# First attention of a four-block fp32 kernel: its heads taken four at a time instead of two, with the product with V split in three

## Chip, core and metric

The kernel runs on one core of a Trainium2 chip. The metric is the device time in microseconds (us), and smaller is better. Every time here is from runs of the kernel, or from one profiled execution of it.

## What is computed

The input x is four sequences of 512 tokens by 512 channels, all fp32. Four residual blocks follow one another: causal attention with 16 heads of 32 channels, a feed-forward with ternary weights, a selective scan, and a last block with a second attention and a mixture of experts. The change is in the first attention:

```python
qkv = jnp.einsum('btc,oc->bto', x, W_qkv).reshape(B, T, 3, H, D)
...
q = _rms_norm(q * cos + _rotate_half(q) * sin)
k = _rms_norm(k * cos + _rotate_half(k) * sin)
scores = jnp.einsum('bhqd,bhkd->bhqk', q, k) * scale
scores = jnp.where(causal[None, None], scores, jnp.float32(-1000000000.0))
attn = jax.nn.softmax(scores, axis=-1)
out = jnp.einsum('bhqk,bhkd->bqhd', attn, v)
out = jnp.transpose(out, (0, 2, 1, 3)).reshape(B, T, C)
return jnp.einsum('btc,oc->bto', out, W_o)
```

## The kernel before, in words

One sequence goes through all layers in a pass of `step`, and there are four passes. Pass 0 has no routed experts to work on; in its place DVE, POOL and the DMA queue turn the feed-forward's weights into ternary ones, from thresholds that need sums over all of those weights. Passes 1 to 3 are one body in a hardware loop; in them the experts of the sequence before run beside the layers of this one. Every engine has its own written-out order of work, and semaphores tie them together. The weights of the q, k and v projection (`wqkv`, 24 KB in each partition) lie in slots 0 and 1 of `ring`; slot 2 holds the shared expert. Once v is there (`v_done`), SP loads the first two routed experts over slots 0 and 1.

The first attention works on pairs of heads, eight pairs (`p`). The heads of a pair lie in two of the four groups of 32 partitions of QT and KT. The scores are transposed (keys in the partitions) and causal: key tile 0 has 512 query columns, tiles 1 to 3 have 384, 256 and 128. They lie in three units: tile 0; tiles 1 and 3; tile 2.

- PE, `pe_A_scores` (L601): for each unit, the matmuls of both heads, each into its own PSUM bank, six banks in all. A unit waits for the exp of the same unit of the pair before.
- ACT (L1620): exp of each unit of two banks into PT, which has room for two pairs.
- POOL, `p_A_select` (L1880): after the third exp it zeroes what lies above the diagonal, in two instructions.
- PE, `pe_A_pv` (L618): the product with V, and with ones for the denominators, of both heads in two column groups, once the select is done. PE does scores of pair p, then the product of pair p-1.
- DVE, `v_A_pair` (L1102 to L1113): transposes the sums, takes reciprocals, and writes two heads to AOT. In pass 0 DVE also has a sum of absolute values of one weight chunk (L1188) after each of the first seven turns.

After the last product PE has, in passes 1 to 3, a part of the shared expert (`pe_E_part`, L910) and then the output projection (`pe_project_A`, L528), which waits for all eight pairs of DVE. In pass 0 the total of the sums (L1158, then the matmul L570 into bank 7) comes before the last product, because the thresholds wait for it; POOL and DVE quantise after it (L1214, L1225).

An fp32 matmul is two instructions on PE here, each with its own weight load (PEld).

```python
for p in range(NP):
    pe_A_scores(pe, p)
    if p:
        pe_A_pv(pe, p - 1)
...
square = PT[:, n % 2].rearrange("p x (k q) -> p (x k) q", q=P)
for blocks in (square[:, 7::12], square[:, 0:21:4]):
```

Of the kernel before, what the change touches and what calls it, by code (L numbers as in the profile page):

```python
# [20 lines left out]
F32 = mybir.dt.float32  # L21
# [8 lines left out]
P = 128  # L30
B, T, C = 4, 512, 512
NT = T // P
# [95 lines left out]
def build(nc, x_in, pack_in, packb_in, wqkv_in, tern_in, exp_in, tern_q, xg, yg, out):  # L128
# [9 lines left out]
    def at(name, shape, dtype, reg, off=0):  # L138
        return nc.alloc_sbuf_tensor_at(name, shape, dtype, offset=offs[reg] + off)
# [77 lines left out]
    STK = at("STK", [P, 4, 2 * GH, 4, HD], F32R, "arena", 40 * KB)  # L217
    QT = at("QT", [P, NK, T], F32, "arena", 24 * KB)
    KT = at("KT", [P, NK, T], F32, "arena", 32 * KB)
    PT = at("PT", [P, 2, 2, 3 * T], F32, "arena", 40 * KB)  # L220
    RA = at("RA", [P, T], F32, "arena", 8 * KB)
    TD = at("TD", [P, T], F32, "arena", 0)
    RDEN = at("RDEN", [P, 16], F32, "arena", 2 * KB)
# [86 lines left out]
    with ExitStack() as ctx:  # L310
# [159 lines left out]
        def tile(i):  # L470
            return slice(i * P, (i + 1) * P)
# [66 lines left out]
        def pe_A(pe, experts):  # L538
            for i in range(NT):
                if i == 1 and experts:  # L540
                    pe_logits(pe)
                if i == 2 and experts:
                    pe_counts(pe)
                if i >= 2:
                    pe.wait_ge(rope_parts, 3 * (i - 1))
                    pe.wait_ge(qk_squared, i - 1)
                pe_A_qkv(pe, i, 0)
                pe_A_qkv(pe, i, 1).then_inc(qk_done, 1)

            for i in range(NT):  # L550
                if i == 1 and experts:
                    pe.wait_ge(r_idx, 1)
                if i >= 2:
                    pe.wait_ge(v_copied, i - 1)
                pe_A_qkv(pe, i, 2).then_inc(v_done, 1)
                if i == 2:
                    for j in range(NT - 1):
                        pe_A_qk(pe, j)
            pe_A_qk(pe, NT - 1)
            for z in range(2):  # L560
                t_emptied(pe, ("qk", NT - 1, z))
            pe.wait_ge(v_copied, NT)
            for p in range(NP):
                pe_A_scores(pe, p)
                if p:
                    pe_A_pv(pe, p - 1)
            if not experts:
                pe.wait_ge(abs_sums, 1)
                pe.wait_ge(a_exp, 3 * NP)
                pe.matmul(ps[:, 7, 0:3], ONES[:], SABS[:], start=True, stop=True).then_inc(thr_sum, 1)  # L570
            pe_A_pv(pe, NP - 1)
            if experts:
                pe.wait_ge(a_exp, 3 * NP)
                pe_E_part(pe, 0, 0, 0, NK)
            else:
                pe.wait_ge(late_loaded, 16)
            pe_project_A(pe)
# [11 lines left out]
        def heads_of(p):  # L589

            g, o = divmod(p, 2)
            return [(4 * g + r, slice(32 * r, 32 * r + 32)) for r in (o, o + 2)]

        def pe_A_scores(pe, p):
            for unit, (_, col, width) in enumerate(A_UNIT):
                if p:
                    pe.wait_ge(a_exp, 3 * (p - 1) + unit + 1)
                for kt in (k for k in range(NT) if A_PLACE[k][0] == unit):
                    off = A_PLACE[kt][1] - col
                    for x, (h, rows) in enumerate(heads_of(p)):  # L600
                        last = pe.matmul(ps[:, 2 + 2 * unit + x, off:off + T - kt * P], KT[rows, h // 4, tile(kt)],  # L601
                                         QT[rows, h // 4, kt * P:T], start=True, stop=True)
                last.then_inc(a_scores, 1)

        def v_ones(h, kt):

            return VA[:, kt, h // 2, h % 2:h % 2 + 2].rearrange("p a d -> p (a d)")

        def pe_A_pv(pe, p):
            if p == 0:  # L610
                pe.wait_ge(ones_a, 1)
            pe.wait_ge(a_sel, p + 1)
            if p >= 2:
                pe.wait_ge(a_head, p - 1)
            for kt in range(NT):
                for x, (h, _) in enumerate(heads_of(p)):
                    col = A_PLACE[kt][1]
                    last = pe.matmul(ps[64 * x:64 * x + 64, p % 2, kt * P:T], v_ones(h, kt),  # L618
                                     PT[:, p % 2, x, col:col + T - kt * P], start=(kt == 0), stop=(kt == NT - 1),
                                     skip_group_check=True)  # L620
            last.then_inc(a_pv, 1)

        def h_bank(m):
            return 2 * (1 - m % 2)
# [472 lines left out]

        def v_A_pair(v, p):

            v.wait_ge(a_pv, p + 1)  # L1100
            odd = p % 2
            v.transpose(TD[:], ps[:, odd]).then_inc(a_recip, 1)  # L1102
            v.wait_ge(a_recip, 3 * p + 1)
            v.reciprocal(RDEN[:], TD[:].rearrange("p (k r) -> p k r", r=32)[:, :, 0]).then_inc(a_recip, 1)
            v.wait_ge(a_recip, 3 * p + 2)
            if p:
                v.wait_ge(a_head, p)
            v.transpose(RA[:].rearrange("p (k r) -> p k r", r=32),
                        RDEN[:].rearrange("p (k o) -> p k o", o=1).to_broadcast([P, 16, 32])).then_inc(a_recip, 1)
            v.wait_ge(a_recip, 3 * p + 3)  # L1110
            for h, rows in heads_of(p):
                den = slice(rows.start + 32 - 64 * odd, rows.stop + 32 - 64 * odd)
                ins = v.tensor_tensor(AOT[rows, h // 4], ps[rows, odd], RA[den], ALU.mult)  # L1113
            ins.then_inc(a_head, 1)

        def v_A(v, experts):
# [481 lines left out]
        def s_A(s, experts):  # L1598
            for i in range(NT):
                b0 = 2 + 3 * (i % 2)  # L1600
                s.wait_ge(qk_done, i + 1)
                if i:
                    s_rms(s, i - 1)
                s.activation(SQ[:], ps[:, b0:b0 + 2, :].rearrange("p b (h d) -> p (b h) d", d=HD),
                             ACT.Square).then_inc(qk_squared, 1)
                if i == 0 and experts:
                    s_route(s)
            s_rms(s, NT - 1)
            for i in range(NT):
                s_v(s, 0, i)  # L1610
                if i == 2:
                    for j in range(NT - 1):
                        s_copy_bank(s, ("qk", j, 0), QT[:, :, tile(j)])
            s_copy_bank(s, ("qk", NT - 1, 0), QT[:, :, tile(NT - 1)])
            for p in range(NP):
                for unit, (_, col, width) in enumerate(A_UNIT):
                    s.wait_ge(a_scores, 3 * p + unit + 1)
                    if p >= 2:
                        s.wait_ge(a_pv, p - 1)
                    s.activation(PT[:, p % 2, :, col:col + width], ps[:, 2 + 2 * unit:4 + 2 * unit, 0:width], ACT.Exp,  # L1620
                                 scale=SCALE).then_inc(a_exp, 1)
            if experts:
                s_tanh(s, 0)
# [251 lines left out]
        def p_A_select(p, n):  # L1875

            p.wait_ge(a_exp, 3 * (n + 1))
            square = PT[:, n % 2].rearrange("p x (k q) -> p (x k) q", q=P)
            for blocks in (square[:, 7::12], square[:, 0:21:4]):
                ins = p.affine_select(blocks, blocks, [[0, blocks.shape[1]], [1, P]], ALU.is_ge, 0.0, base=0, channel_multiplier=-1)  # L1880
            ins.then_inc(a_sel, 1)

# [25 lines left out]
        def p_A(p, link, experts):  # L1908
            p.memset(VA[:, :, :, 1], 1.0).then_inc(ones_a, 1)
            if experts:  # L1910
                p_scatter(p)
            for n in range(NP):
                p_A_select(p, n)
            if not experts:
                for m in range(2):
                    p_below(p, m)
            for i in range(NT):
                p_rstd(p, link, 1, i)
            if not experts:
                for m in range(2, NM):  # L1920
                    p_below(p, m)
# [161 lines left out]
        def step(x_next, out_batch, experts):  # L2083
# [10 lines left out]
            with nc.Block() as block:  # L2094
                @block.sync
                def _(sp):
# [5 lines left out]
                            n = min(NT, NB - b)  # L2102
                            sp.dma_start(rows[:, b:b + n], XS[:, 0:n]).then_inc(zeros_sent, 16)
                    if experts:
                        sp.wait_ge(v_done, NT)
                        for b in range(2):
                            load_gate_up(sp, b, exp_in[b + 1])
                            load_down(sp, b, exp_in[b + 1])
                        sp.wait_ge(a_pv, NP)
                        for m in range(NM):  # L2110
                            load_tern(sp, m)
                        xs_all_sent(sp)
                        sp.wait_ge(e_up, 2)
# [20 lines left out]
                    else:  # L2134
                        sp.dma_start(ring[:, 2], exp_in[0]).then_inc(next_loaded, 16)
                        load_next(sp)
                        sp.wait_ge(next_loaded, 16)
                    if experts:
                        sp.wait_ge(stored, 16)
                        sp.wait_ge(wqkv_loaded, 16)  # L2140
                    sp.wait_ge(x_loaded, 16 * NT)

                @block.tensor
# [189 lines left out]
```

## Time and profile before

| what | us |
| --- | --- |
| median of 3 runs (2122.47 to 2124.69) | 2123.91 |
| the profiled execution, its own time | 2125.45 |
| span of its instructions | 2123.7 |
| PE busy | 1885.2 (89%) |
| DVE busy | 1377.2 (65%) |
| ACT busy | 994.7 (47%) |
| POOL busy | 786.7 (37%) |
| mean granted TensorE clock | 0.928 |

Times in the trace count from the start of the span. PE is TensorE's matmuls, PEld its weight loads, DVE VectorE, ACT ScalarE, POOL GpSimd, SP the engine that issues DMAs. What stands in brackets behind a row is the idle time of its engine before it, and who ended it. A granted clock of 1.0 is 2.4 GHz, and 0.5 is 1.2 GHz. The first attention's scores begin at 67.5 us in pass 0 and at 568.7 us in pass 1.

### The profile page before, as it was taken

The numbers are of one execution on the slowest core, as the hardware profiler recorded it, in microseconds if no ns is written. First come the engines' busy times: TensorE is split into PE (matmuls) and PEld (weight loads), VectorE is DVE, ScalarE is ACT, GpSimd is POOL, SyncE is SP. The second block draws the span as 40 slices with busy tenths as digits, with TensorE's granted clock in tenths as the row PEclk, the third lists the DMA queues.
The fourth block names the chain that finished last, engine by engine and source line by source line (L and its number), as shares of the span: only waits on it lengthen the run. The fifth ranks groups of instructions, "written<-read, shape, count | busy, mean of one in ns | idle before, by whom it ended". The sixth has DMA issues, their size and how long they took to land. (4 is left out here: it accounts for less than half of the span.)

```text
span 2123.7 us, 27520 instructions
## 1 busy us (share of the span) xinstructions
PE 1885.2 (89%) x9226; PEld 1238.9 (58%) x9226; DVE 1377.2 (65%) x2196; ACT 994.7 (47%) x1736; POOL 786.7 (37%) x1057
## 2 busy tenths in 40 slices
PE   7878665998999899997999899898899999899895
PEld 3446443695458565695447555496446666588442
DVE  5766698574563799574664699577554499667411
ACT  1412774462322786363232698264142399355021
POOL 1146377441210276561120177372020157472201
PEclk9989755998999999998999999999899999899898
DMA  6337100000213185200213176210022257310683
GB/s 259 109 115 245 52 0 20 1 2 1 99 45 119 57 266 173 96 25 22 79 51 119 35 244 227 84 41 21 17 97 93 69 175 263 127 41 21 237 311 104
DMA packets 55072, 221.09 MB, mean 104 GB/s; under 512 B 6288, under 2 KB 6288, under 8 KB 46992
## 3 DMA queue, kind: packets, MB, share of 16 engines
q1 hardware_dynamic: 45776, 195.14, 26.5%
q0 software_dynamic: 5120, 16.78, 2.4%
q10 hardware_dynamic: 4032, 7.34, 0.9%
q8 instruction: 80, 1.31, 0.3%
q14 instruction: 64, 0.52, 0.1%
HBM read 179.65 MB, written 39.58 MB: 103 GB/s over the span
## 5 line engine op out<-in xcount | busy, mean ns | idle before, releaser
L1933 POOL TENSOR_TENSOR Y<-Y,HC 128x1024 f32<-128x1024 f32 x116 | 273.9, 2362 | 174.0 <-DVE HC L1336 173.4
L1325 DVE TENSOR_TENSOR_SCAN HS<-DA,ps 128x1024 f32<-128x1024 f32 x128 | 292.3, 2284 | 23.5 <-PE ps L742 13.0
L534 PE MATMUL ps<-ring,XNT 128*128 128x512 f32 x384 | 182.4, 633 | 21.0 <-issue 12.2
L1688 ACT ACTIVATE DA<-DL,AB,AN 128x511 f32<-128x511 f32 x256 | 193.8, 806 | 14.8 <-DVE HS L1325 13.5
L954 PE MATMUL ps<-ring,XBT 128*128 128x512 f32 x384 | 188.5, 597 | 0.0
L1801 ACT ACTIVATE PD<-ps,NMX 128x128 f32<-128x128 f32 (+3 forms) x256 | 135.1, 530 | 101.2 <-DVE NMX L1470 99.2
L1470 DVE TENSOR_REDUCE NMX<-ps 128x1 f32<-128x128 f32 (+3 forms) x256 | 124.3, 487 | 65.4 <-PE ps L805 65.1
L823 PE MATMUL ps<-V,PTD 128*128 128x33 f32 x1280 | 164.2, 262 | 0.0
L823 PEld LDWEIGHTS ps<-V,PTD 128*128 128x128 f32 x1280 | 162.6, 192 | 0.5 <-ACT PTD L839 0.5
L650 PE MATMUL ps<-XNH,tern 128*128 128x512 f32 x352 | 139.2, 396 | 9.8 <-DVE tern L1225 5.4
L534 PEld LDWEIGHTS ps<-ring,XNT 128*128 128x128 f32 x384 | 76.6, 204 | 117.4 <-issue 108.1
L1336 DVE TENSOR_TENSOR HC<-HS,ps 128x1024 f32<-128x1024 f32 x120 | 143.2, 1196 | 0.0
L650 PE MATMUL ps<-XNL,tern 128*128 128x512 f32 x352 | 137.9, 392 | 0.0
L1847 POOL TENSOR_SCALAR RS<-MV 128x1 f32<-128x1 f32 x32 | 12.8, 399 | 291.7 <-DVE MV L1039 291.7
L1872 POOL TENSOR_TENSOR STK<-QN,STK 128x128 fp32r<-128x128 f32 x256 | 116.4, 476 | 10.3
L1868 POOL CAST STK<-QN 128x128 fp32r<-128x128 f32 x256 | 67.9, 295 | 139.4 <-DVE QN L1460 90.5
L814 PE MATMUL ps<-pack,PD 128*128 128x128 f32 x640 | 113.4, 275 | 4.3 <-ACT XNT L1082 4.3
L742 PE MATMUL ps<-pack,UBE 128*128 128x128 f32 x512 | 84.5, 320 | 26.1 <-DVE HS L1325 22.8
L1620 ACT ACTIVATE PT<-ps 128x1024 f32<-128x1024 f32 (+1 forms) x96 | 77.3, 886 | 57.0 <-PE ps L601 57.0
L803 PE MATMUL ps<-QKS 128*128 128x128 f32 (+3 forms) x256 | 99.8, 392 | 3.1 <-ACT QKS L1076 3.1
L1880 POOL TENSOR_SCALAR_AFFINE_SELECT PT<-PT 128x256 f32<-128x256 f32 x64 | 39.3, 638 | 169.8 <-ACT PT L1620 169.8
L742 PE MATMUL ps<-pack,UBO 128*128 128x128 f32 x512 | 81.4, 313 | 21.6 <-DVE HS L1325 20.5
(248 smaller groups left out, 4026.0 us busy)
## 6 DMA issues: line engine op xcount, KB each, us to landing
ring<-experts_dram SPq DMA_DIRECT2D x48, 1024.0 KB, 5.1
tern<-tern_q SPq DMA_DIRECT2D x33, 768.0 KB, 4.2
ring<-experts_dram SPq DMA_DIRECT2D x48, 512.0 KB, 5.4
RAW<-tern_dram SPq DMA_DIRECT2D x22, 768.0 KB, 4.8
ring<-wqkv_dram SPq DMA_DIRECT2D x4, 3072.0 KB, 11.9
XB<-xg SPq DMA_DIRECT2D x42, 256.0 KB, 3.6
yg<-YB SPq DMA_DIRECT2D x42, 256.0 KB, 4.9
tern_q<-tern SPq DMA_DIRECT2D x11, 768.0 KB, 7.0
```

The lines of the kernel that those rows point to most:

```text
L534: last = pe.matmul(ps[:, 2 + 3 * (i % 2) + part], XNT[:, k, tile(i)], wqkv[:, k, part * C:(part + 1) * C], start=(k == 0), stop=(k == NK - 1))
L650: last = pe.matmul(ps[:, h_bank(m) + n], tern[:, m % 3, w:w + P], parts[a][:, k], start=(k + a == 0), stop=(k == NK - 1 and a == 1))
L742: last = pe.transpose(ps[:, 2 * q + jj, tile(i)], ub(n, i)[:, tile(2 * q + jj)], ident)
L823: last = pe.matmul(ps[:, 6 + h % 2, 33 * i:33 * i + 33], PTD[:, v % 3, tile(kt)], V1[:, kt, h], start=(kt == 0), stop=(kt == i))
L954: last = pe.matmul(ps[:, g_bank(b)], XBT[:, b % 2, k], weights(b)[:, k * C:(k + 1) * C], start=(k == 0), stop=(k == NK - 1), skip_group_ch ...
L1325: v.tensor_tensor_scan(HS[:, q].rearrange("p j t -> p (j t)"), DA[:, q].rearrange("p j t -> p (j t)"), ps[:, 2 * q:2 * q + 2].rearrange("p ...
L1336: v.tensor_tensor(dst, HS[:, q], ps[:, 4:5, :].to_broadcast([P, 2, T]), ALU.mult).then_inc(c_hc, 1)
L1470: v.tensor_reduce(NMX[:, u % 4:u % 4 + 1], ps[:, 2 + u % 3, 0:(i + 1) * P], AX.X, ALU.max, negate=True).then_inc(d_max, 1)
L1688: s.activation(DA[:, u % 2, jj, 1:T], DL[:, j, 1:T], ACT.Exp, scale=AN[:, j * NS + n:j * NS + n + 1], bias=AB[:, j * NS + n:j * NS + n + 1 ...
L1801: s.activation(PD[:, u % 3, 0:(i + 1) * P], ps[:, 2 + u % 3, 0:(i + 1) * P], ACT.Exp, bias=NMX[:, u % 4:u % 4 + 1]).then_inc(d_exp, 1)
L1872: p.tensor_tensor(st[:, :, LOW[z]], qn, st[:, :, HIGH[z]].bitcast(F32), ALU.subtract).then_inc(stack_ready, 1)
L1933: p.tensor_tensor(y, y, HC[:, q], ALU.add).then_inc(c_y, 1)
```

## The change

The unit of work becomes a quad of four heads (`g`, four quads), in all four groups of partitions. The scores of one unit go to the four banks 2 to 5, and all three units share these banks, so each unit waits for the exp of the unit before it. The exps work on four banks at a time. The product with V of quad g-1 is cut by unit and set between the score units of quad g; it goes to banks 6 and 7 or 0 and 1 in turn. The select of a quad is four instructions, after its third exp. DVE still works by pairs, but gets two pairs at once. PT becomes two buffers of 24 KB; the second lies in slots 0 and 1 of `ring`. So the first two experts are loaded later (behind the third chunk of ternary weights), and pass 0 loads `wqkv` again at its end. The total of the absolute sums in pass 0 comes after the last product.

```diff
-    PT = at("PT", [P, 2, 2, 3 * T], F32, "arena", 40 * KB)
+    PT = (at("PT0", [P, 4, 3 * T], F32, "arena", 40 * KB), at("PT1", [P, 4, 3 * T], F32, "ring"))
...
-            for p in range(NP):
-                pe_A_scores(pe, p)
-                if p:
-                    pe_A_pv(pe, p - 1)
+            for g in range(NK + 1):
+                for unit in range(len(A_UNIT)):
+                    if g < NK:
+                        pe_A_scores(pe, g, unit)
+                    if g:
+                        pe_A_pv(pe, g - 1, unit)
             if not experts:
                 pe.wait_ge(abs_sums, 1)
-                pe.wait_ge(a_exp, 3 * NP)
+                pe.wait_ge(a_head, NP - 2)
                 pe.matmul(ps[:, 7, 0:3], ONES[:], SABS[:], start=True, stop=True).then_inc(thr_sum, 1)
-            pe_A_pv(pe, NP - 1)
             if experts:
-                pe.wait_ge(a_exp, 3 * NP)
+                pe.wait_ge(a_head, NP - 2)
                 pe_E_part(pe, 0, 0, 0, NK)
...
+        def a_bank(g):
+            return 6 * (1 - g % 2)
+
+        def pe_A_scores(pe, g, unit):
+
+            if g or unit:
+                pe.wait_ge(a_exp, 3 * g + unit)
+            _, col, width = A_UNIT[unit]
+            for kt in (k for k in range(NT) if A_PLACE[k][0] == unit):
+                off = A_PLACE[kt][1] - col
+                for r in range(4):
+                    rows = slice(32 * r, 32 * r + 32)
+                    last = pe.matmul(ps[:, 2 + r, off:off + T - kt * P], KT[rows, g, tile(kt)],
+                                     QT[rows, g, kt * P:T], start=True, stop=True)
+            last.then_inc(a_scores, 1)
...
+        def pe_A_pv(pe, g, unit):
+            if unit == 0:
+                if g == 0:
+                    pe.wait_ge(ones_a, 1)
+                pe.wait_ge(a_sel, g + 1)
+                if g >= 2:
+                    pe.wait_ge(a_head, 2 * (g - 1))
+            for kt in (k for k in range(NT) if A_PLACE[k][0] == unit):
+                for o in range(2):
+                    for x in range(2):
+                        col = A_PLACE[kt][1]
+                        last = pe.matmul(ps[64 * x:64 * x + 64, a_bank(g) + o, kt * P:T], v_ones(4 * g + o + 2 * x, kt),
+                                         PT[g % 2][:, o + 2 * x, col:col + T - kt * P], start=(kt == 0), stop=(kt == 2),
+                                         skip_group_check=True)
+            if unit == len(A_UNIT) - 1:
+                last.then_inc(a_pv, 1)
...
-            v.wait_ge(a_pv, p + 1)
+            v.wait_ge(a_pv, p // 2 + 1)
...
-                    s.activation(PT[:, p % 2, :, col:col + width], ps[:, 2 + 2 * unit:4 + 2 * unit, 0:width], ACT.Exp,
+                    s.activation(PT[g % 2][:, :, col:col + width], ps[:, 2:6, 0:width], ACT.Exp,
...
-            for blocks in (square[:, 7::12], square[:, 0:21:4]):
+            for blocks in (square[:, 7::12], square[:, 0::12], square[:, 4::12], square[:, 8::12]):
...
                     if experts:
-                        sp.wait_ge(v_done, NT)
-                        for b in range(2):
-                            load_gate_up(sp, b, exp_in[b + 1])
-                            load_down(sp, b, exp_in[b + 1])
-                        sp.wait_ge(a_pv, NP)
+                        sp.wait_ge(a_pv, NK)
                         for m in range(NM):
+                            if m == 3:
+                                for b in range(2):
+                                    load_gate_up(sp, b, exp_in[b + 1])
+                                    load_down(sp, b, exp_in[b + 1])
                             load_tern(sp, m)
...
                         load_next(sp)
+                        sp.dma_start(wqkv[:], wqkv_in.rearrange("p (k n) -> p k n", k=NK)).then_inc(wqkv_loaded, 16)
```

## Rows read from the trace of the kernel before

**Rows 1.** The page's busy times: engine, us, share of the span, instructions.

```profile
PE 1885.2 (89%) x9226; PEld 1238.9 (58%) x9226; DVE 1377.2 (65%) x2196; ACT 994.7 (47%) x1736; POOL 786.7 (37%) x1057
```

**Rows 2.** Timeline, pass 1, one pair: start, us, engine, line, operation [idle before].

```profile
585.35 2.43 PE L601 MATMUL ps<-QT,KT 32*128 32x512 f32 x16
...
586.53 2.43 ACT L1620 ACTIVATE PT<-ps 128x1024 f32<-128x1024 f32 x3 [2.23 <-PE ps L601]
...
587.71 2.37 PE L618 MATMUL ps<-PT,VA 128*64 128x512 f32 x16
...
589.02 1.23 POOL L1880 TENSOR_SCALAR_AFFINE_SELECT PT<-PT 128x256 f32<-128x256 f32 x2 [3.44 <-ACT PT L1620]
...
590.02 2.43 PE L601 MATMUL ps<-QT,KT 32*128 32x512 f32 x16
```

**Rows 3.** Groups by form, pass 1, 568 to 611 us: busy us, mean ns | idle before.

```profile
L1620 ACT ACTIVATE PT<-ps 128x1024 f32<-128x1024 f32 x16 | 15.5, 1025 | 14.2 <-PE ps L601 14.2
...
L1880 POOL TENSOR_SCALAR_AFFINE_SELECT PT<-PT 128x768 f32<-128x768 f32 x8 | 6.9, 866 | 0.0
...
L1620 ACT ACTIVATE PT<-ps 128x512 f32<-128x512 f32 x8 | 4.9, 608 | 0.0
...
L601 PE MATMUL ps<-QT,KT 32*128 32x256 f32 x32 | 4.8, 376 | 0.0
...
L1880 POOL TENSOR_SCALAR_AFFINE_SELECT PT<-PT 128x256 f32<-128x256 f32 x8 | 3.3, 410 | 31.7 <-ACT PT L1620 31.7
...
L601 PE MATMUL ps<-QT,KT 32*128 32x128 f32 x32 | 3.1, 269 | 0.0
```

**Rows 4.** Timeline, pass 1, the first two pairs' scores.

```profile
568.68 4.72 PE L601 MATMUL ps<-QT,KT 32*128 32x512 f32 x32 [0.83 <-DVE KT L1082]
```

**Rows 5.** Timeline, pass 1, the end of the first attention.

```profile
604.12 0.72 DVE L1102 STREAM_TRANSPOSE TD<-ps 128x512 f32<-128x512 f32 x1 [1.48 <-PE ps L618]
...
606.59 3.70 PE L910 MATMUL ps<-XET,ring 128*128 128x512 f32 x8
...
607.32 0.72 DVE L1102 STREAM_TRANSPOSE TD<-ps 128x512 f32<-128x512 f32 x1
...
610.55 10.57 PE L528 MATMUL ps<-pack,AOT 128*128 128x512 f32 x24 [0.26 <-DVE AOT L1113]
```

**Rows 6.** Timeline, pass 0, DVE and PE.

```profile
74.96 0.72 DVE L1102 STREAM_TRANSPOSE TD<-ps 128x512 f32<-128x512 f32 x1 [5.79 <-PE ps L618]
...
105.60 0.72 DVE L1102 STREAM_TRANSPOSE TD<-ps 128x512 f32<-128x512 f32 x1
...
108.80 0.19 DVE L1158 TENSOR_REDUCE SABS<-SPART 128x3 f32<-128x33 f32 x1
...
113.60 0.72 DVE L1102 STREAM_TRANSPOSE TD<-ps 128x512 f32<-128x512 f32 x1 [3.25 <-PE ps L618]
...
116.92 13.53 PE L528 MATMUL ps<-pack,AOT 128*128 128x512 f32 x24 [3.45 <-DVE AOT L1113]
```

**Rows 7.** Timeline of PE: three places where it had been idle.

```profile
716.01 0.66 PE L712 MATMUL ps<-pack,U 128*128 128x128 f32 x4 [2.66 <-DVE U L1285]
...
883.26 1.50 PE L495 MATMUL ps<-pack,STK 128*128 128x128 f32 x12 [1.62 <-DVE M L1455]
...
1484.05 0.66 PE L488 MATMUL ps<-pack,XS 128*128 128x128 f32 x4 [2.21 <-DVE XS L1046]
```

**Rows 8.** Stretches: us, busy times (instructions) by engine, granted clock, DMA share, GB/s.

```profile
716.90:727.10 10.20, 8.03 (x36) 7.41 (x37) 6.83 (x4) 10.17 (x19) 1.71 (x2) 0.50 0.09 23
...
1485.00:1498.00 13.00, 5.65 (x10) 2.65 (x11) 1.44 (x2) 2.20 (x3) 1.10 (x2) 0.50 0.02 6
...
883.00:897.00 14.00, 11.05 (x92) 9.71 (x92) 8.80 (x20) 7.40 (x15) 12.11 (x31) 1.00 0.14 40
256.00:370.00 114.00, 65.58 (x255) 48.99 (x256) 106.34 (x75) 73.58 (x112) 84.49 (x51) 0.50 0.03 10
```

**Rows 9.** Stretch in which the first two experts are loaded, pass 1; columns as above.

```profile
572.00:575.00 3.00, 2.68 (x22) 1.38 (x22) 0.00 (x0) 2.60 (x4) 1.57 (x3) 1.00 1.03 425
```

More of the change, by code:

```diff
@@ L592, in heads_of @@
             return [(4 * g + r, slice(32 * r, 32 * r + 32)) for r in (o, o + 2)]
[L594 to L603, printed above, removed]
+        def a_bank(g):
+            return 6 * (1 - g % 2)
@@ L605, in v_ones @@
         def v_ones(h, kt):
             return VA[:, kt, h // 2, h % 2:h % 2 + 2].rearrange("p a d -> p (a d)")
[L609 to L621, printed above, removed]
+        def pe_A_pv(pe, g, unit):
[14 more added lines that the diff above has]
+                last.then_inc(a_pv, 1)
@@ L1098, in v_A_pair @@
         def v_A_pair(v, p):
-            v.wait_ge(a_pv, p + 1)
+            v.wait_ge(a_pv, p // 2 + 1)
             odd = p % 2
-            v.transpose(TD[:], ps[:, odd]).then_inc(a_recip, 1)
+            bank = a_bank(p // 2) + odd
+            v.transpose(TD[:], ps[:, bank]).then_inc(a_recip, 1)
             v.wait_ge(a_recip, 3 * p + 1)
@@ L1112, in v_A_pair @@
                 den = slice(rows.start + 32 - 64 * odd, rows.stop + 32 - 64 * odd)
-                ins = v.tensor_tensor(AOT[rows, h // 4], ps[rows, odd], RA[den], ALU.mult)
+                ins = v.tensor_tensor(AOT[rows, h // 4], ps[rows, bank], RA[den], ALU.mult)
             ins.then_inc(a_head, 1)
@@ L1614, in s_A @@
             s_copy_bank(s, ("qk", NT - 1, 0), QT[:, :, tile(NT - 1)])
-            for p in range(NP):
+            for g in range(NK):
                 for unit, (_, col, width) in enumerate(A_UNIT):
-                    s.wait_ge(a_scores, 3 * p + unit + 1)
-                    if p >= 2:
-                        s.wait_ge(a_pv, p - 1)
-                    s.activation(PT[:, p % 2, :, col:col + width], ps[:, 2 + 2 * unit:4 + 2 * unit, 0:width], ACT.Exp,
+                    s.wait_ge(a_scores, 3 * g + unit + 1)
+                    if g >= 2:
+                        s.wait_ge(a_pv, g - 1)
+                    s.activation(PT[g % 2][:, :, col:col + width], ps[:, 2:6, 0:width], ACT.Exp,
                                  scale=SCALE).then_inc(a_exp, 1)
@@ L1877, in p_A_select @@
             p.wait_ge(a_exp, 3 * (n + 1))
-            square = PT[:, n % 2].rearrange("p x (k q) -> p (x k) q", q=P)
-            for blocks in (square[:, 7::12], square[:, 0:21:4]):
+            square = PT[n % 2][:].rearrange("p x (k q) -> p (x k) q", q=P)
+            for blocks in (square[:, 7::12], square[:, 0::12], square[:, 4::12], square[:, 8::12]):
                 ins = p.affine_select(blocks, blocks, [[0, blocks.shape[1]], [1, P]], ALU.is_ge, 0.0, base=0, channel_multiplier=-1)
@@ L1911, in p_A @@
                 p_scatter(p)
-            for n in range(NP):
+            for n in range(NK):
                 p_A_select(p, n)
@@ L2139, in _ @@
                         sp.wait_ge(stored, 16)
-                        sp.wait_ge(wqkv_loaded, 16)
+                    sp.wait_ge(wqkv_loaded, 16)
                     sp.wait_ge(x_loaded, 16 * NT)
```

## The prediction

> **What bounds the kernel now.** I read the page's busy times first: PE is busy for 89% of the span, so it is the engine to watch [rows 1]. Then I read the timeline of one pair in pass 1, where the reader is to see a closed loop on PE: scores begin at 585.35, the product with V at 587.71, the next scores at 590.02, with no idle time [rows 2]. A pair takes 4.67 us, four heads take 9.33, and ACT waits 2.23 us in each pair for PE. The exps (2.43 us) and the select (1.23 us) run under PE's work. So cheaper scores can pay only if what hides behind them stays hidden. The groups by form give the prices [rows 3], the rows at the stage's two ends show what PE waits for after it [rows 4, 5], and pass 0 is a case of its own: from 74.96 to 105.60 DVE works through six turns of 5.11 us without waiting, so there DVE is the bound, and the thresholds and the last pair follow it [rows 6].
>
> **Prices.** 128 more columns cost an fp32 scores matmul 376 - 269 = 107 ns, for each of its two instructions [rows 3]. A head has 1280 columns, so two heads side by side need 10 x 2 x 0.107 = 2.14 us. Scores took 2.36 and the product 2.31 [rows 2], so each change between the two array shapes costs about 0.2. ACT sees a 512-column unit 1.18 us after its first matmul [rows 2], and a 256-column one after some 0.75 (0.1 shape, 0.21 first instruction, 0.38 the last one's own time, 0.05 signal). Exp costs 608 ns for 512 elements and 1025 for 1024 [rows 3]: 0.81 per 1000 and 0.19 fixed, so 1.86 for four banks of 512 (a quad's first two units) and 1.02 for the third. Select costs 410 ns for 256 elements and 866 for 768 [rows 3], so 0.64 for 512; four of them, overlapping as now, take 2.45.
>
> **Scores in four row groups.** The trace shows two groups side by side and not four. Bounds: four cost what two cost (2.14 a quad instead of 4.28), or they run as two and two (4.28). I take the first, since the second head now adds nothing that shows. On this the Trainium skill speaks against the full gain: "TensorE: Matmul & The Clock Gate", section "Measured speedup vs the span model", gives 3.07 times for four row tiles of K=32, N=512. An estimate from that page's figure is scores 1.30 times as long, 0.7 us a quad, 11 us over the kernel; no row here shows it, and the sum leaves it out.
>
> **The new cycle.** The three score units share four banks, so exp and scores alternate. Let an exp chain of a quad end at 0. At 0.05 the next quad's first scores start, and their exp starts at 1.23 and ends at 3.09. The select of the old quad runs from 0.06 to 2.51. PE has its scores done at 1.0 and then stands before the product until 2.55, because that waits for the whole select, which nothing covers now. The product's first part ends at 4.3 (two banks x 2 x 0.43, and 0.05). Scores of unit 1 are queued behind it: 4.4, exp from 5.58 to 7.44. Product part 2 lies beside that exp (5.4 to 7.2). Scores of unit 2 start at 7.5, exp 8.25 to 9.27. The cycle is 9.3 us against 9.33 before: **the 2.14 us that scores save are given back** to the select (1.5), the exp waits (0.3) and two more shape changes (0.4).
>
> **The ends of the stage.** Quad 0 has no product beside it: 3.04, 3.09 and 1.8 us for its three units, 7.95 in all. Three cycles follow, to 35.8. Then the last select, bare, to 38.3. Then a whole quad's product, 4.28 + 0.1: 42.7. DVE gets pairs 6 and 7 together; a pair takes 607.32 - 604.12 = 3.20 [rows 5], so the last head is there at 42.7 + 0.2 + 6.4 = 49.3. Before, the projection began 610.55 - 568.68 = 41.9 after the first scores [rows 4, 5]. **The stage ends 7.4 us later**, in passes 1 to 3. The shared expert's part (3.7 us, rows 5 show it beside the last pair) fills less of the wait. I take 7.3, as ideal joins may lose or save 0.1.
>
> **Clock.** What PE did before its clock fell: after idle times of 2.66 and 2.21 us it stood at 0.50 (1.2 GHz) for the next 10.2 and 13 us; after one of 1.62 between dense work it stayed at 1.00 (2.4 GHz) [rows 7, 8]. The new stage has such idle times at three places that had none. (a) Quad 0: 2 us, 2 us and 1 us with about 1 us of work between. Price: nothing, up to 5 (10.2 us at half); PE's waits absorb part, and I take 1.4. (b) Before the last product: PE's work ended at 35.6, so 2.7 us idle, as the row that fell: the product's 4.4 us become 8.6, +4.2 (bounds 0 and 5.1). (c) Before the projection: PE is through with the expert's part at about 51.6, DVE at 53.5; 1.9 us lie between the row that fell and the one that did not, so I take half of 5.1, 2.5.
> Passes 1 to 3: 7.3 + 1.4 + 4.2 + 2.5 = 15.4 each, 46.2.
>
> **Pass 0.** DVE has nothing to do until the first quad's product is done, at 17.0 + 0.2 + 1.4 (a): 67.5 + 18.6 = 86.1 in place of 74.96, and its queue is in order, so the sums of later chunks wait too. Six turns of 5.11 end at 116.8, pair 6 at 120.0; sum, its matmul and thresholds 1.5 (the same work as before, now with pair 7 behind it), pair 7: 124.7. Before, pair 7 started at 113.60 and ended at 116.8. +7.9. The projection is slow there already (24 matmuls in 13.53 us against 10.57 [rows 5, 6]), so its clock adds nothing. The quantising waits for thresholds that come 11 us later, but its second chunk ends by 132, as the first residual add would start: hidden, up to 1.
>
> **DMA and the rest.** The first two experts, 3 MB, now follow the third ternary chunk; they moved at 425 GB/s [rows 9], so 8 us. The fourth chunk, queued behind them on SP, is asked for only after the first down product; in the code two norms, two up products and that one lie between, longer than the 8 us. Cost 0, and if that cover went, up to 3 a pass. The experts themselves are needed only in the scan. The second load of wqkv has the last attention of pass 0 over it: 0. Addresses and banks: 0.
>
> **Sum.** 46.2 + 7.9 = 54.1. The profiled execution took 2125.45, so it would be 2179.6; it stands 1.5 above the median of 2123.91, and against that I say **2178**.
>
> **Rivals.**
> - *Schedule only, no fall of the clock.* 3 x 7.3 + 6.5 = 28.4: 2152. For it: score bursts in quad 0 may count as work. Against: idle times over 2.2 us were followed by 0.50 in both rows.
> - *Four groups run as two and two.* The change would not do what it says. Every 512-column unit is 0.43 later; by the same steps the stage is 6 longer (3.4 in pass 0, where only the first two quads count): +21, 2199.
> - *The clock stays low through the stage,* as in pass 0's scan, at 0.50 for 114 us with PE busy 58% [rows 8]. Product and scores at half, 14.5 a quad: about 20 more a pass: 2240. Against: at half speed PE has hardly a gap left, and there it recovers.
> - *Faster.* One mechanism: the shift in time takes away low-clock stretches elsewhere, such as those after 716 and 1484 us [rows 8], each worth 5.1 to 6.5. The stage alone loses 28 even without new falls (a cycle below 6.9 us would be needed to break even, and PE's own work is 7.6), so it takes six stretches gone and none new: about 2117 with seven. I know of no reason why.
> - *Select much cheaper and no fall:* with 1.2 us in place of 2.45 the cycle is 8.1 and the end 1.2 earlier: 4.8 less a pass, 2135. Even that is slower.
>
> **How the numbers follow.** Forecast 0.55 (its own range 2160 to 2196), schedule only 0.2, two and two 0.1, low throughout 0.05, cheap select 0.03, faster 0.05, no change 0.02. The range goes from 2143, below schedule only, to 2205, above two and two. A difference under 0.2% (4 us) can't be told from none here. Faster 0.05, same 0.02, slower 0.93.
>
> **What would show it.** Right: PE rows of a quad 9.3 us apart; idle of 1.5 us before the first product part, ended by POOL; 2.7 us before the last; scores of a quad begun within 30 ns in four groups; exps of 1.86; DVE pairs 6 and 7 back to back and the projection 49 us or more after the first scores; granted clock 0.50 over the last product. In pass 0, thresholds some 11 us later. Wrong: a cycle under 8.5, a select under 1.5 in all, or the clock at 1.00 through the stage's end (then 2152).

## The result, and the profile after

The changed kernel is slower: median 2164.77 us of four runs (2162.29 to 2170.81) against 2123.19 of the kernel before, ratio 1.0205 with a 95% interval of 1.0177 to 1.0233 (the two medians alone give 1.0196). So that it is slower is clear, and whether by more than 2% is not. The profiled execution has a span of 2169.0 us against 2123.7, so 45.3 more.

| first scores to start of projection, us | before | after | forecast |
| --- | --- | --- | --- |
| pass 0 | 49.4 | 57.2 | +7.9 |
| pass 1 | 41.9 | 52.2 | +15.4 less 2.5 (c, in the projection) |
| pass 2 | 41.9 | 53.8 | the same |
| pass 3 | 41.8 | 53.8 | the same |

These four lines hold 42.0 of the 45.3: 7.8 + 10.3 + 11.9 + 12.0. The rest lies outside (the first scores 1.3 later in pass 0; from each projection to the next pass's scores +3.3, +3.4 and -4.8; the end +0.1). The -4.8 says little of the change: the kernel before itself took 446.4 us there in pass 1 and 452.8 in pass 2, and its low-clock stretches lie differently in the two.

The page's busy times answer to [rows 1]. PE is busy for 9 us less, yet the span is 45 longer.

```profile
PE 1876.5 (87%) x9226; PEld 1222.6 (56%) x9226; DVE 1378.0 (64%) x2196; ACT 993.9 (46%) x1688; POOL 783.6 (36%) x1057
```

One cycle of a quad, in the timeline of pass 2 after the change; it answers to [rows 2].

```profile
1103.06 1.14 PE L607 MATMUL ps<-QT,KT 32*128 32x512 f32 x8
1103.07 2.40 POOL L1890 TENSOR_SCALAR_AFFINE_SELECT PT<-PT 128x512 f32<-128x512 f32 x4 [8.87 <-ACT PT L1630]
...
1104.27 1.88 ACT L1630 ACTIVATE PT<-ps 128x2048 f32<-128x2048 f32 x1 [1.26 <-PE ps L607]
...
1105.53 1.94 PE L626 MATMUL ps<-PT,VA 128*64 128x512 f32 x8 [1.33 <-POOL PT L1890]
...
1107.39 1.15 PE L607 MATMUL ps<-QT,KT 32*128 32x384 f32 x16
...
1108.47 1.95 PE L626 MATMUL ps<-PT,VA 128*64 128x384 f32 x16
1108.61 1.88 ACT L1630 ACTIVATE PT<-ps 128x2048 f32<-128x2048 f32 x1 [2.47 <-PE ps L607]
...
1110.54 0.71 PE L607 MATMUL ps<-QT,KT 32*128 32x256 f32 x8
1111.18 1.08 PE L626 MATMUL ps<-PT,VA 128*64 128x256 f32 x8
...
1112.40 1.14 PE L607 MATMUL ps<-QT,KT 32*128 32x512 f32 x8
```

Read it from the first line: eight matmul instructions, four heads, are done in 1.14 us, and their exp starts 1.21 us after the first of them has begun, where with two heads it was 1.18 [rows 2]. The first four matmul instructions, one of each head, begin within 20 ns (1103.059 to 1103.079). So all four row groups ran side by side. Then look at the bracket before the first product: PE stood 1.33 us for POOL's select, which takes 2.40. The next quad starts 9.34 us after this one; two pairs took 9.33. The gain on scores is gone within the cycle.

The end of the stage in the same pass; it answers to [rows 5].

```profile
1121.65 0.72 DVE L1112 STREAM_TRANSPOSE TD<-ps 128x512 f32<-128x512 f32 x1 [2.96 <-PE ps L626]
1121.75 2.40 POOL L1890 TENSOR_SCALAR_AFFINE_SELECT PT<-PT 128x512 f32<-128x512 f32 x4 [6.94 <-ACT PT L1630]
...
1124.20 6.22 PE L626 MATMUL ps<-PT,VA 128*64 128x512 f32 x32 [2.60 <-POOL PT L1890]
...
1130.35 3.70 PE L919 MATMUL ps<-XET,ring 128*128 128x512 f32 x8
1130.47 0.72 DVE L1112 STREAM_TRANSPOSE TD<-ps 128x512 f32<-128x512 f32 x1 [2.44 <-PE ps L626]
...
1133.67 0.72 DVE L1112 STREAM_TRANSPOSE TD<-ps 128x512 f32<-128x512 f32 x1
...
1136.90 3.27 PE L528 MATMUL ps<-pack,AOT 128*128 128x512 f32 x7 [2.85 <-DVE AOT L1123]
```

The last select is bare (2.60 idle), the last product takes 6.22 us, then DVE's pairs 6 and 7 follow one another, and PE waits 2.85 for them. What PE waited for in the whole run (waiting line, releaser: us, times, longest):

```profile
PE ps L626 <- POOL PT L1890: 23.0, 16, 2.6
PE ps L607 <- ACT PT L1630: 20.5, 12, 2.0
```

The product waited for the select 16 times, once a quad. Before, both of its engines together (PE and its weight loads) had waited 3.3 us for it, in ten places.

The granted clock of four stretches of pass 2 (columns as in [rows 8]): quad 0; the three cycles; the last product; the projection.

```profile
1083.00:1092.00 9.00, 3.76 (x36) 1.81 (x40) 0.01 (x1) 5.60 (x4) 0.21 (x1) 0.77 0.01 2
1098.00:1123.00 25.00, 20.32 (x177) 9.15 (x176) 13.50 (x23) 12.46 (x8) 6.05 (x11) 1.00 0.00 1
1123.00:1131.00 8.00, 6.80 (x34) 2.98 (x35) 5.37 (x9) 0.00 (x0) 1.15 (x2) 0.79 0.01 2
1136.90:1147.00 10.10, 10.10 (x24) 4.60 (x25) 4.25 (x8) 0.00 (x0) 1.80 (x4) 1.00 0.00 0
```

The clock fell in quad 0 and in the last product, and not in the projection, though PE had been idle 2.85 us ahead of it. In pass 1 it was the other way: the last product took 4.53 us, and the projection's three tiles 12.26 in place of 10.57 [rows 5].

### The profile page after: what moved, and what is told of

Read it like the earlier page. It is cut to its first block and busy times, and to the rows that moved or that the text cites. A ratio compares the mean times of both kernels' runs of the same rounds, so it can differ in the third digit from the quotient of the medians.

```text
span 2169.0 us, 27409 instructions
## 1 busy us (share of the span) xinstructions
PE 1876.5 (87%) x9226; PEld 1222.6 (56%) x9226; DVE 1378.0 (64%) x2196; ACT 993.9 (46%) x1688; POOL 783.6 (36%) x1057
## 5 line engine op out<-in xcount | busy, mean ns | idle before, releaser
L1882 POOL TENSOR_TENSOR STK<-QN,STK 128x128 fp32r<-128x128 f32 x256 | 116.3, 476 | 10.3
L1630 ACT ACTIVATE PT<-ps 128x2048 f32<-128x2048 f32 (+1 forms) x48 | 76.5, 1593 | 73.7 <-PE ps L607 73.7
L626 PE MATMUL ps<-PT,VA 128*64 128x256 f32 (+3 forms) x512 | 88.4, 486 | 23.0 <-POOL PT L1890 23.0
L1890 POOL TENSOR_SCALAR_AFFINE_SELECT PT<-PT 128x512 f32<-128x512 f32 x64 | 38.4, 638 | 192.4 <-ACT PT L1630 192.4
```

What stands on the lines that cost most here:

```text
L1882: p.tensor_tensor(st[:, :, LOW[z]], qn, st[:, :, HIGH[z]].bitcast(F32), ALU.subtract).then_inc(stack_ready, 1)
```

## The experiments

### The select, by unit

```diff
-            p.wait_ge(a_exp, 3 * (n + 1))
             square = PT[n % 2][:].rearrange("p x (k q) -> p (x k) q", q=P)
-            for blocks in (square[:, 7::12], square[:, 0::12], square[:, 4::12], square[:, 8::12]):
-                ins = p.affine_select(...)
-            ins.then_inc(a_sel, 1)
+            for unit, offs_ in enumerate(((0,), (4, 7), (8,))):
+                p.wait_ge(a_exp, 3 * n + unit + 1)
+                for off in offs_:
+                    blocks = square[:, off::12]
+                    ins = p.affine_select(...)
+                ins.then_inc(a_sel, 1)
...
-                pe.wait_ge(a_sel, g + 1)
+            pe.wait_ge(a_sel, 3 * g + unit + 1)
```

> The changed kernel with its select cut by score unit: POOL masks unit 0 right after the first exp, the others after theirs, and each third of the product waits for its own select. Theory (the bare select of 2.4 us holds PE before the first third of the product, and the exp chain is the next limit): the cycle of a quad falls from 9.34 us to 8.0, the idle before the first third (1.33) goes, the idle of 2.6 before the last product falls to 0.7 or less; then DVE is late next, with pairs 4 to 7 back to back after the third quad's product, so the projection comes 4.5 to 6 us earlier in passes 1 to 3, and 1.3 in pass 0: some 18 us less than the change, ratio to the kernel before 1.012. Rival (the exp chain and the shape changes alone set 9.3): the cycle stays above 9, and less than 4 us are gained.

Measured: 2149.84 us, ratio 1.0122 (1.0100 to 1.0144). In passes 1 to 3 the projection starts 48.6 us after the first scores, 3.6 to 5.2 less than in the changed kernel. The timeline of pass 2:

```profile
1089.17 1.14 PE L607 MATMUL ps<-QT,KT 32*128 32x512 f32 x8
1090.24 1.94 PE L626 MATMUL ps<-PT,VA 128*64 128x512 f32 x8
...
1097.31 1.14 PE L607 MATMUL ps<-QT,KT 32*128 32x512 f32 x8
...
1105.37 0.72 DVE L1112 STREAM_TRANSPOSE TD<-ps 128x512 f32<-128x512 f32 x1 [1.76 <-PE ps L626]
...
1108.57 0.72 DVE L1112 STREAM_TRANSPOSE TD<-ps 128x512 f32<-128x512 f32 x1
...
1111.77 0.72 DVE L1112 STREAM_TRANSPOSE TD<-ps 128x512 f32<-128x512 f32 x1
1111.80 5.37 PE L919 MATMUL ps<-XET,ring 128*128 128x512 f32 x8 [2.17 <-DVE AOT L1123]
...
1114.97 0.72 DVE L1112 STREAM_TRANSPOSE TD<-ps 128x512 f32<-128x512 f32 x1
```

The product follows its scores with no idle time, the cycle is 8.14 us, and DVE now works through four pairs without a pause. The theory holds, its ratio of 1.012 too, and the rival falls: the bare select is 1.2 us of each cycle and more at the end. What is late next is DVE. The falls of the clock are still there (13.7 us at 0.50 in each of these stages); one makes the shared expert's part take 5.37 us in place of 3.70.

### Idle time filled with unread matmuls

```diff
+        def pe_fill(pe, n, bank):
+            for _ in range(n):
+                pe.matmul(ps[:, bank], KT[:, 0, tile(0)], QT[:, 0], start=True, stop=True)
...
+                    if g == 0:
+                        pe_fill(pe, (2, 2, 1)[unit], 7)
+                    if g == NK and unit == 0:
+                        pe.wait_ge(a_exp, 3 * NK)
+                        pe_fill(pe, 2, 2)
```

> The changed kernel with matmuls that nobody reads in PE's idle time: two after each of the first two score units of quad 0, one after the third, and two before the last product. They fit in the idle times (0.86 us each in 2.0, 2.0, 1.1 and 2.6 us), so the order and every wait stay. Theory (the idle times let the clock fall, and that costs 3 us in quad 0 and up to 1.7 before the last product, a pass): granted clock 1.00 over the whole stage, the projection 49.3 us after the first scores in place of 52.2 and 53.8, 3 to 4.6 us a pass and about 1 to 3 in pass 0, together 12 to 16 us less than the change: ratio 1.014. Rival (the clock falls in spite of them, or they push the chain): no gain, or 1 to 2 us more a pass.

Measured: 2162.73 us, ratio 1.0177 (1.0148 to 1.0207). Of the 12 to 16 us expected, 2 came by the medians and some 6 by the ratios, so the forecast of 1.014 missed. The stage did nearly what was forecast, 49.7 us in passes 1 to 3 in place of 52.2 and 53.8, with the clock at 1.00 in quad 0 and full speed in the last product; pass 0 gave 1.0. But the clock now fell over the projection in each of passes 1 to 3. Stretches of pass 2, quad 0 and projection, and the rows of the end:

```profile
1078.70:1088.00 9.30, 9.02 (x50) 3.30 (x50) 0.00 (x0) 5.48 (x4) 1.16 (x2) 1.00 0.01 2
1128.40:1138.00 9.60, 9.60 (x19) 4.37 (x20) 3.14 (x6) 0.00 (x0) 0.79 (x2) 0.84 0.00 0
```

```profile
1117.40 4.53 PE L635 MATMUL ps<-PT,VA 128*64 128x512 f32 x32 [0.48 <-POOL PT L1899]
1121.85 3.70 PE L928 MATMUL ps<-XET,ring 128*128 128x512 f32 x8
1128.40 12.05 PE L528 MATMUL ps<-pack,AOT 128*128 128x512 f32 x24 [2.85 <-DVE AOT L1132]
```

The last product takes 4.53 us in place of 6.22, so that fall cost 1.7; the projection's three tiles take 12.05 in place of 10.57 [rows 5]. In passes 1 to 3 of this kernel and of the changed one, then, a fall at the stage's end was paid once, at one place or the other.

### The third place filled too

```diff
                 pe_E_part(pe, 0, 0, 0, NK)
+                pe_fill(pe, 3, 2)
```

> As the second experiment, with three more unread matmuls after the shared expert's part, in the 2.85 us in which PE waits for DVE's last pair. Theory (each pass pays for one fall at the end of the stage, before the last product or, when that is kept busy, before the projection): no fall there either in passes 1 to 3, the projection's three tiles in 10.6 us instead of 12.1, 1.5 us a pass less than with the two places filled: ratio 1.0155. Rival (the projection's clock does not depend on that idle time): as before, 1.018.

Measured: 2162.63 us, ratio 1.0181 (1.0153 to 1.0209). In place the theory holds: with 0.27 us of idle time ahead of it the projection ran at full clock.

```profile
1126.55 2.74 PE L603 MATMUL ps<-QT,KT 128*128 128x512 f32 x6
1129.56 10.57 PE L528 MATMUL ps<-pack,AOT 128*128 128x512 f32 x24 [0.27 <-DVE AOT L1133]
```

The total did not move, so the 1.0155 expected did not come. From the start of the work after the projection on, the stretch to the next pass's scores has more low-clock time than with two places filled (44.4 us in passes 1 and 2, against 34.1 and 27.3) and is longer (431.8 us in both, against 430.4 and 427.4). So the local gain was lost again in stretches of low clock elsewhere.

### The loads alone, on the kernel before

```diff
-                        sp.wait_ge(v_done, NT)
-                        for b in range(2):
-                            ...
                         sp.wait_ge(a_pv, NP)
                         for m in range(NM):
+                            if m == 3:
+                                for b in range(2):
+                                    load_gate_up(sp, b, exp_in[b + 1])
+                                    load_down(sp, b, exp_in[b + 1])
```

The second load of `wqkv` in pass 0, with its wait, is in this kernel too.

> The kernel before with the DMA part of the change alone: the first two experts are loaded behind the third ternary chunk, and pass 0 loads wqkv again. Theory: nothing waits for either, ratio 1.000, within 0.2%. Rival (the fourth ternary chunk is late behind 3 MB): PE idle before the fourth up product ended by the DMA, 1 to 3 us in each of passes 1 to 3, ratio up to 1.004.

Measured: 2124.05 us, ratio 0.9995 (0.9976 to 1.0014). The DMA part of the change costs nothing that can be measured.

### Sums of pass 0 ahead of the first pair

```diff
-                if not experts and NT + p < NM:
-                    v_abs_sums(v, NT + p)
+                if not experts:
+                    for m in (range(NT, NT + 4) if p == 0 else range(NT + 3 + p, min(NT + 4 + p, NM))):
+                        v_abs_sums(v, m)
```

> The changed kernel, but in pass 0 DVE does four sums of weight chunks before it waits for pair 0, in place of one, and the others after the pairs as before. Theory (in pass 0 DVE is the bound from the first quad's product on, and its sums queue behind that wait): three sums of 1.87 us go into the 16.8 us in which DVE idles; thresholds, the last pair and the projection of pass 0 come 5.6 us earlier, the other passes stay: ratio 1.018. Rival (PE or the weight chunks' loads bound pass 0): under 1 us.

Measured: 2159.32 us, ratio 1.0152 (1.0128 to 1.0177). The stage of pass 0 went from 57.2 us to 53.8, 3.4 of the 5.6 expected. DVE's rows say why it is not more:

```profile
110.70 0.72 DVE L1112 STREAM_TRANSPOSE TD<-ps 128x512 f32<-128x512 f32 x1
114.63 0.72 DVE L1112 STREAM_TRANSPOSE TD<-ps 128x512 f32<-128x512 f32 x1 [0.75 <-PE ps L626]
```

With the sums out of the way, pair 6 waits for PE's last product. DVE was the bound, as the theory has it, but with only 3.4 us to the next one. The median fell by some 5 us, and by the ratios, each against the kernel before timed beside it, it is some 11; what is more than the 3.4 has no place in the stage, and the intervals of the two ratios just touch.

### The last quad, pair by pair

The product of quad 3 is taken over all key tiles for its first pair, then for its second, with a signal after each; DVE's pair 7 waits for the second.

> The changed kernel, the product of the last quad alone taken pair after pair (four key tiles of one pair, then of the other), with a signal after each. Theory (DVE gets pairs 6 and 7 together, and that is 3.2 us of the later end): pair 6 starts when pair 5 is through, 0.8 us earlier where the last product ran at full clock and up to 2.5 where it fell, nothing in pass 0: 2 to 6 us less than the change, ratio 1.018 to 1.0195. Rival (the last pair waits for PE, not for DVE): 0.

Measured: 2170.80 us, ratio 1.0222 (1.0192 to 1.0252), so no gain in total. The stage did shrink by what was expected, 0.8 us in pass 1, 2.2 and 2.5 in passes 2 and 3. Against it, the clock was low for 17.1 us of pass 0's stage up to its last product, in place of 10.2; DVE's first pair came 20.8 us after the first scores in place of 18.5, and the stage was 2.3 longer. The passes' remainders (from a projection's start on) changed by -2.0, +3.7, -0.6 and +2.4 us. Pairs in twos cost what was said; the total can't show it.

### Quads with all of it mended

Select by unit, a product cut so that the first pair of a quad is complete in its second slot, a signal for each pair, filled idle time in quad 0, and the sums early:

```diff
+            for o, kt in (((0, 0), (0, 1)), ((0, 3), (0, 2), (1, 0)), ((1, 1), (1, 3), (1, 2)))[slot]:
...
+                if kt == 2:
+                    last.then_inc(a_pv, 1)
```

> Quads with everything mended that was found: select by unit; the product of a quad cut so that its first pair is complete in the second slot, with a signal for each pair; unread matmuls in quad 0's idle time; three more sums of pass 0 done before the first pair. Theory (what quads lost was the bare select, the late start of DVE, the pairs in twos and the clock): DVE's chain of eight pairs from 12.9 us on with the last at 41.6, against 41.9 in the kernel before, and 4 us less in pass 0: ratio 0.998, between 0.996 and 1.002. Rival (quad 0 alone, 8 us without a product, keeps quads behind): 1.004 or more.

Measured: 2135.03 us, ratio 1.0043 (1.0026 to 1.0059), the best with quads and still slower than the kernel before, as the rival has it; the theory's 0.998 missed. The clock is at 1.00 in the stage of passes 1 to 3, and it takes 43.0 us against 41.9.

```profile
1062.90:1105.90 43.00, 38.97 (x274) 16.33 (x274) 24.45 (x41) 20.43 (x14) 10.00 (x16) 1.00 0.10 36
```

```profile
1076.18 0.72 DVE L1117 STREAM_TRANSPOSE TD<-ps 128x512 f32<-128x512 f32 x1 [13.37 <-PE ps L631]
...
1084.55 0.72 DVE L1117 STREAM_TRANSPOSE TD<-ps 128x512 f32<-128x512 f32 x1 [1.84 <-PE ps L631]
...
1092.93 0.72 DVE L1117 STREAM_TRANSPOSE TD<-ps 128x512 f32<-128x512 f32 x1 [1.84 <-PE ps L631]
...
1102.69 0.72 DVE L1117 STREAM_TRANSPOSE TD<-ps 128x512 f32<-128x512 f32 x1
...
1105.92 10.57 PE L528 MATMUL ps<-pack,AOT 128*128 128x512 f32 x24 [1.75 <-DVE AOT L1128]
```

DVE's first pair comes 13.3 us after the first scores (1062.9), where pairs had it at 7.5 (74.96 - 67.5 in pass 0 of the kernel before). Eight pairs of 3.2 us, two waits of 1.84 and three of 0.19 do the rest. That is the rival's mechanism, and it is 1.1 us a pass. Pass 0's stage is 46.3 us against 49.4. By the four stages the kernel would be level with the one before (0.3 us more in all). The rest of the 9.6 us by which its profiled execution is behind is outside the stages: the first scores 1.5 later, and the four remainders +1.1, +5.2, -0.8 and +2.2 us. The -0.8 is again against the long pass 2 of the kernel before; against the kernel with the loads alone, passes 1 and 2 are 5.3 and 5.4 longer. The second fall that the last section shows is in both, and makes up 3.7 and 4.0 of that; it was not tried by itself.

### The kernel before, its sums early

The same edit of DVE's order with two sums more ahead of the first pair, on pairs.

> The kernel before (pairs) with two more sums of pass 0 done before pair 0. Theory (in pass 0 of the kernel before, DVE's turns of 5.11 us are slower than PE's 4.67, and DVE idles 5.8 us before the first): the turns become as fast as PE's, thresholds and the last pair come 2.5 us earlier, ratio 0.999. Rival: the chunks' loads are late and nothing moves.

Measured: 2118.51 us, ratio 0.9980 (0.9959 to 1.0000). Pass 0's stage went from 49.4 us to 46.5. Run again in more rounds:

> The same kernel as in the eighth experiment, timed in more rounds, to tell a gain of 0.1 to 0.2% from none. Theory: ratio 0.998 to 0.999. Rival: 1.000.

Measured: 2118.47 us, ratio 0.9967 (0.9945 to 0.9988). This version beats the kernel before by 0.2 to 0.3%, and is the fastest of all those here. The stage of pass 0 (46.7 us in this profiled execution) shows 2.7 to 2.9 us of it, 0.13%; no place was found for the rest.

### Unread matmuls at the end of a pass

```diff
             for i in range(2, NT):
+                for _ in range(4 - i):
+                    pe.matmul(ps[:, 6], ident, wo[:, 0], start=True, stop=True)
                 pe_norm(pe, 4, i)
```

> The kernel of the ninth run, with unread matmuls at the end of each pass: two in PE's idle time of 2.21 us before the third transposition of the last norm, one before the fourth. Theory (what a low stretch costs depends on where it falls: here it covers the next pass's projection of q, k and v, which PE bounds): the stretch of 13.65 us at 1.2 GHz that now begins at those transpositions does not begin there; it is shorter or gone and 1 to 5 us a pass come back, ratio 0.992 to 0.997. Rival (the idle time of 5.9 us at the border of the passes, which these cannot fill, makes the clock fall by itself, only later): the low time moves further into the projection of q, k and v, and the ratio is that of the ninth run or up to 0.003 above it.

Measured: 2120.27 us, ratio 0.9989 (0.9966 to 1.0011), not told apart from the run without them. The clock did not fall at the transpositions. It fell some 7 us later: at 996.8, within the idle time of 5.84 us at the passes' border, so that the projection of q, k and v (from 998.5) began at half speed, and at the end of pass 1 it fell once more after that. Stretches of the end of pass 1:

```profile
990.00:996.80 6.80, 2.17 (x10) 1.11 (x10) 2.13 (x3) 1.17 (x2) 2.00 (x3) 1.00 0.02 5
996.80:1003.70 6.90, 5.23 (x7) 2.18 (x8) 0.00 (x0) 1.28 (x1) 0.00 (x0) 0.51 0.02 6
1003.70:1010.50 6.80, 6.80 (x35) 4.41 (x33) 1.27 (x2) 1.02 (x1) 0.00 (x0) 0.99 0.01 2
1010.50:1017.40 6.90, 6.90 (x16) 4.07 (x17) 5.96 (x26) 1.51 (x2) 0.00 (x0) 0.51 0.00 0
```

That fits the rival's account: the idle time at the border is enough for the fall. At the end of pass 2 the low time was 6.8 us in place of 13.7, with no second fall, and the remainder of the pass was no shorter (446.5 us against 446.4 in the ninth run).

## Why the prediction was right, point by point

The direction and the range held, and the size roughly: 54.1 us forecast; measured were 41.6 by the medians, 43 by the ratio and 45.3 by the profiled executions. The schedule without the clock was forecast at 29.8 and came to 31.3 (7.8 in pass 0, 7.8 in each other pass); the clock in passes 1 to 3 was forecast at 24.3 and came to 12.4. So the mechanism was right, and one term was twice too large. By its own steps:

- **Scores in four row groups.** Right: four cost what two cost. The estimate from the figure in the Trainium skill ("TensorE: Matmul & The Clock Gate", "Measured speedup vs the span model") would have put the exp some 0.26 us later (0.30 of 0.86); it came 0.03 later, so this trace does not show that cost. The estimate took the page's 3.07 for four tiles as if two tiles lost nothing beside one, which no run here shows. Leaving it out of the sum was right.
- **The cycle.** Forecast 9.3, measured 9.34. The product's wait was 1.33 (forecast 1.5), the exp of four banks 1.88 (1.86), the select 2.40 (2.45). That the select is the cause was argued then; the first experiment shows it, 9.34 to 8.14 with the select by unit.
- **The ends.** Forecast 7.3 later. With the clock kept up by filled idle time the stage took 49.7 us, 7.8 later. The idle time before the last product was 2.60 (2.7).
- **The clock.** This is the term that was mis-sized, 8.1 us a pass forecast for three places: 2.5 of them in quad 0 (I said 1.4), from 52.2 - 49.7 in pass 1; 1.6 in the last product in passes 2 and 3 and nothing in pass 1 (I said 4.2 everywhere); 1.7 in the projection in pass 1 and nothing in passes 2 and 3 (I said 2.5). So 4.1 to 4.2 a pass. The step that failed is "as the row that fell": I took a fall of 10.2 us from the row whose idle time was like it. At the stage's end the falls lasted 3.4 us, and only one of the two idle times brought one.
- **Pass 0.** Forecast +7.9, measured +7.8, by DVE's late start: its first pair came 18.5 us after the first scores (forecast 18.6). The thresholds came at 122.7 in place of 110.3, 12.4 later (forecast some 11), and from the projection's start to the feed-forward's first products it took 0.1 more: hidden, as said.
- **DMA.** Forecast 0, measured 0.9995 for it alone.
- **The rivals.** "Two and two", "low throughout" and "faster" did not come. "Schedule only" did not either, but the truth lies between it (2152) and the forecast (2178), near the middle. The price of "cheap select" was slightly off: 4.8 less in three passes and 1.2 in pass 0 gives 2136 to 2138, not 2135.
- **What I had no term for.** The remainders of the passes moved by -4.8 to +3.4 us each, and with the first scores they add 3.3 us to the span. None of the shifts is larger than the 6.4 us between the remainders of passes 1 and 2 within the kernel before.

## What to carry to other kernels

When a stage is widened so that one engine does more at once, write down what each other engine now gets only in bulk: here a mask after the last of three exps, and the normalisations of two pairs at a time, each of which had been hidden behind the work that was made cheaper. Cut the follow-up work at the same places as the work it follows, and signal it piece by piece. And where an engine waits at a stage's start, see whether its queue holds work that could go first; two such sums took 2.7 to 2.9 us off pass 0's stage with no other change, in a kernel that came out 0.2 to 0.3% faster.

## What the runs showed of the hardware that I had not expected

The clock can fall while PE is busy without a break, some time after an idle stretch, even if it had been at full level in between. At the border of the first two expert passes PE was idle for 6.16 us from 1018.8 on and worked from 1025.0; the stretches of the changed kernel that follow:

```profile
1016.30:1029.90 13.60, 6.19 (x12) 2.90 (x11) 1.59 (x3) 2.46 (x3) 1.53 (x2) 0.50 0.02 5
1030.00:1036.70 6.70, 6.70 (x33) 4.21 (x31) 1.05 (x1) 1.02 (x1) 0.00 (x0) 1.00 0.00 0
1036.80:1043.50 6.70, 6.70 (x17) 4.12 (x18) 6.07 (x27) 1.51 (x2) 0.00 (x0) 0.50 0.00 0
```

0.50 (1.2 GHz), 1.00 (2.4 GHz), and 0.50 again with PE busy for all of the last two. In the kernel with the select by unit, with the same work at the same place, the clock stayed up:

```profile
1006.10:1019.50 13.40, 6.79 (x14) 3.41 (x15) 2.12 (x3) 2.46 (x3) 1.97 (x3) 0.50 0.02 6
1019.60:1035.00 15.40, 15.40 (x73) 8.85 (x73) 7.23 (x27) 2.68 (x4) 0.00 (x0) 1.00 0.00 1
```

From the start of the projection of q, k and v to the next scores it took 58.1 to 58.6 us at borders with the second fall and 54.3 to 54.7 at those without, so the fall costs 3.7. It came at some borders and not at others, within one kernel too. The kernel before has it at the end of pass 2 and not at the end of pass 1:

```profile
1498.70:1505.20 6.50, 6.50 (x33) 4.11 (x31) 1.01 (x1) 1.02 (x1) 0.00 (x0) 1.00 0.00 0
1505.40:1512.00 6.60, 6.60 (x17) 4.02 (x17) 6.02 (x27) 1.51 (x2) 0.00 (x0) 0.50 0.01 2
```

The length of the idle time does not part the two kinds: 5.80 us with a second fall (two places filled, end of pass 1), 6.41 without (the loads alone, end of pass 2). What parts them in the traces is the moment at which work came back. In the eleven profiled executions without matmuls put in at this border, at the ends of passes 1 and 2, the projection began 7.9 to 8.8 us after the clock's first fall at all ten borders where a second followed, and 8.9 to 9.6 us after it at all twelve where none did. This was read afterwards, and no experiment here varied that moment alone, so the cause stays open. The second fall is a likely part of why the gain in place of the last quad pair by pair did not show in the total; with the third place filled it came at both borders, with two filled at one. A change of this size has to be judged by place in the trace as well as by its total.
